# Two-branch image kernel: the first unit's second half moves from GpSimd to VectorE, and the last unit's residual into the output sums

## The chip, the cores and the metric

One NeuronCore of one Trainium2 chip runs the whole kernel. The metric is device time in microseconds (us): the time from the start to the end of one execution. In the profile PE is TensorE (PEld its weight load), DVE is VectorE, ACT is ScalarE, POOL is GpSimd, SP is the engine that issues most of the DMAs; a q behind a name means that engine's queue or sequencer.

## The reference

The input x is (4, 96, 128, 128) in float32. Two residual steps follow each other, each on a group-normalised copy (32 groups of 3 channels):

```
x = x + L0(gn(x))   # layer norm over channels, 1x1 q/kv, depthwise 3x3, channel attention, 1x1 projection
x = x + L1(gn(x))   # 1x1, 3x3, 5x5 and dilated 3x3 convolutions, concatenated, 1x1 fuse back to 96 channels
```

The second step is linear between the norm and the sum. The kernel folds its five weights into one 5x5 convolution of 96 by 96 channels. gn(v) is (v - m) / sqrt(s + eps), m and s being the mean and variance of a group over the image.

## The kernel before

The four images run one after the other. For each image the phases are: projection of the normed rows (L772, float32 matmuls), depthwise convolution as band matrices (L793 to L795), gram products and softmax, the attention output (L855) added to X by DVE (L1432), the statistics of the new X, and then the folded 5x5 convolution in 11 units of rows (L924, L919). X, the image in float32, lies in SBUF all the time.

The convolution is a fast (Toom-Cook-like) form: a unit is 12 rows (4 blocks of 3; the last unit has 8 rows), and its rows are turned into five "points" (planes of a block, two column kinds each) by differences of rows. The points are 4, 3, 1, 0 and 2 in the order of the matmuls. Points 3 and 4 are the first half ("part 0" in the code), points 0, 1 and 2 the second half ("part 1"). For each half there are the planes themselves ("plain") and sums of neighbouring columns ("sums"). Each value is split into a high float16 part (made by ACT, function highs, L1122 and L1127, copied once more by L1116 and L1117) and a low float16 part (made by DVE, lows, L1554 for unit 0 and L1557 for the others). DMAs then place the low parts in further partitions: place_first (L371 to L374, L360 to L362) for unit 0, copy_block (L384) and place_low (L440 to L443, L360 to L362) for the later ones.

Unit 0 is special, since it waits for the second group norm. The mean and variance come from sums over the image: DVE's additions L1432 give the sum, ACT's squares L1085 the sum of squares. Then a chain of single-column instructions on DVE, two 96x1 matmuls on PE (L753: the mean over a group, then the variance) and a root on ACT (L962) give the scale SA and shift SBI (L1487, L1488). So as not to wait for them, the row differences of unit 0 are made from X itself before the scale is known (a difference of rows needs no mean), and the scale enters when the halves are rounded to float16. Who makes them before the change:

- POOL (first_planes, helper take at L632 and column_sums at L628) makes the differences and all points of blocks 1 to 4, first half and second half, and the column sums. Then, once DVE has laid the rows of block 0 less their mean (first_block_rows, L1445, counted in s_pl0), POOL makes the second half of block 0 too. s_fp counts POOL's steps, 24 an image.
- DVE makes block 0's first half (L1450, L1455), adds twice the mean back to the one plane where it doesn't cancel (L1460) and makes the remaining column sums (L1465, L1468).
- ACT then rounds: part 0 plain when s_pl0 is at 4, part 0 sums at s_pl0 6 and s_fp 11, part 1 plain at s_fp 23, then the copies of part 0, part 1 sums at s_fp 24, the normed rows of unit 1 (rows_normed, L1103), and the copies of part 1.
- DVE makes the low parts of part 0 (plain, sums) and part 1 (plain, sums), the x3 and x1 of line L1554. SP places part 0 after the second of them and part 1 after the fourth.
- PE starts unit 0 when its high parts (s_h at 5) and part 0's placed tiles are there.

Next DVE makes unit 1's points (planes: L1511, L1508, L1518, L1519, L1514, L1515, L1536), which needs ACT's normed rows, and its low parts, which need all of unit 0's placing DMAs to be done (s_firstp, s_firstlo), as its buffer is reused. Unit 1's first point on PE leaves its matmuls with the placed low parts for last (L919); they wait for place_low's DMAs.

From unit 2 on DVE, ACT, POOL (differences, L680), SP and PE run in a loop of windows, one unit each. A unit's output: ACT copies the first point (L1166), DVE adds the others from PSUM into acc with their factors (first_rows L1587, last_rows L1605; s_acc counts 11 steps a unit), then adds pairs of kinds into the output buffer ob (outputs, L1618: first the middle row, then the outer rows), POOL adds X (residual, L670, counted in s_res), and SP writes ob out (write_out, L452). The middle outputs wait until the write of the unit before has landed (s_out). After the last unit the next image's projection begins on PE with nothing between.

## Time and profile before

| what | value |
|---|---|
| median of 3 runs | 1725.4 us (1724.74 to 1725.86) |
| profiled execution's own time | 1725.26 us |
| its span | 1723.0 us |
| PE, DVE, ACT, POOL busy | 96%, 87%, 59%, 37% of the span |
| granted TensorE clock, mean | 0.975 of full |

The profile shows one execution. Its span is the time from the first to the last instruction or DMA; the device time is 2.3 us more. Times in rows are us from the start of the span. A number in brackets at a row's end is the time that the engine sat idle before it, with what ended that idle time.

### The profile page before, as it was taken

How to read it: one execution, taken by the hardware profiler on the slowest of the kernel's cores; microseconds unless marked ns; L12 is line 12 of the kernel's file. 1: busy time of each engine (PE TensorE's matmuls, PEld its weight loads, DVE VectorE, ACT ScalarE, POOL GpSimd, SP SyncE). 2: the span in 40 equal slices, each digit the busy share in tenths (PEclk: the TensorE clock that was granted, in tenths of full speed). 3: DMA queues.
4: the chain of work that ended last, by engine and by line, in shares of the span. 5: the costliest groups of instructions: out<-in, count | busy, mean ns of one | idle time of the engine just before them, and what ended most of it. 6: DMA issues, size and time to landing. Idle time of an engine off the chain costs nothing.

```text
span 1723.0 us, 39391 instructions
## 1 busy us (share of the span) xinstructions
PE 1645.8 (96%) x13285; PEld 1550.5 (90%) x13285; DVE 1492.8 (87%) x1930; ACT 1011.6 (59%) x1647; POOL 637.2 (37%) x446
## 2 busy tenths in 40 slices
PE   6999989999999997999999999899999999899998
PEld 5989959999999994999999996799999999599998
DVE  6798879999788859999978886999987887799996
ACT  2866667455285657645546666655447565765541
POOL 5799962222381005232247003323227400512232
PEclk9999979999999998999999998899999999799999
DMA  7012115666502201566630220366651121055553
GB/s 190 0 42 61 45 31 126 169 165 171 148 19 57 72 19 39 149 168 177 165 99 14 73 60 1 86 164 174 168 159 46 41 69 38 1 137 132 140 146 95
DMA packets 101181, 166.05 MB, mean 96 GB/s; under 512 B 40010, under 2 KB 74411, under 8 KB 100940
## 3 DMA queue, kind: packets, MB, share of 16 engines
q1 hardware_dynamic: 77932, 138.95, 31.8%
q10 hardware_dynamic: 23168, 26.04, 4.8%
q8 instruction: 47, 0.77, 0.2%
q14 instruction: 34, 0.28, 0.1%
HBM read 52.20 MB, written 25.17 MB: 45 GB/s over the span
## 4 chain that ended last, share of the span: by engine, by line
PE 70%; DVE 12%; issue 11%; ACT 3%; POOL 1%; SPq 1%; DMA 1%; DVEq 1%; ACTq 0%; POOLq 0%
PE ps L924 28%; PE ps L772 12%; PE ps L793 8%; PE ps L795 7%; PE ps L794 7%; PE ps L821 3%; PE ps L855 3%; DVE region L1557 1%; DVE region L1587 1%; DVE region L1508 1%; POOL region L670 1%; PE ps L735 1%; DVE region L1605 1%; PE ps L919 1%; DMA region<-region 1%
## 5 line engine op out<-in xcount | busy, mean ns | idle before, releaser
L924 PE MATMUL ps<-region,W 128*96 128x256 f16 (+4 forms) x7156 | 796.7, 270 | 5.7 <-DMA region<-region 5.7
L924 PEld LDWEIGHTS ps<-region,W 128*96 128x96 f16 (+2 forms) x7156 | 774.9, 122 | 20.6 <-issue 14.1
L1346 DVE TENSOR_TENSOR region<-V,band 128x2322 f32<-128x2322 f32 (+2 forms) x104 | 257.7, 2488 | 59.2 <-PE ps L795 56.1
L1122 ACT ACTIVATE region<-region 96x1584 f16<-96x1584 f32 (+1 forms) x80 | 98.1, 1273 | 311.0 <-DVE region L1519 306.2
L680 POOL TENSOR_TENSOR region<-region 96x528 f32<-96x528 f32 (+1 forms) x72 | 96.4, 1344 | 407.8 <-DVE region L1557 405.8
L793 PE MATMUL ps<-region 128*128 (+1 forms) x1152 | 228.2, 280 | 10.0 <-DVE region L1355 4.4
L795 PE MATMUL ps<-region 128*128 (+1 forms) x1152 | 222.8, 275 | 0.0
L794 PE MATMUL ps<-region 128*128 (+1 forms) x1152 | 222.3, 275 | 0.0
L1587 DVE SCALAR_TENSOR_TENSOR region<-ps,small,region 96x768 f32<-96x768 f32 (+1 forms) x220 | 203.7, 988 | 10.3 <-PE ps L924 8.5
L772 PE MATMUL ps<-proj,region 96*128 96x240 f32 x1024 | 210.1, 368 | 0.5 <-DVE region L1605 0.4
L772 PEld LDWEIGHTS ps<-proj,region 96*128 96x128 f32 x1024 | 195.2, 191 | 14.4 <-issue 1.2
L670 POOL TENSOR_TENSOR region<-region,X 96x1536 f32<-96x1536 f32 (+1 forms) x44 | 124.0, 2818 | 225.2 <-DVE region L1618 225.2
L793 PEld LDWEIGHTS ps<-region 128*128 128x128 f32 x1152 | 174.6, 192 | 16.5 <-issue 14.8
L599 POOL TENSOR_TENSOR region<-region,cbias 128x576 f32 (+1 forms) x124 | 175.7, 1417 | 34.8 <-DVE region L1320 30.6
L1557 DVE TENSOR_TENSOR region<-region 96x792 f16<-96x792 f32 (+6 forms) x160 | 175.1, 1153 | 0.9 <-DMA region<-region 0.8
L795 PEld LDWEIGHTS ps<-region 128*128 128x128 f32 x1152 | 174.9, 192 | 0.0
L794 PEld LDWEIGHTS ps<-region 128*128 128x128 f32 x1152 | 174.9, 192 | 0.0
L632 POOL TENSOR_TENSOR region<-X 96x512 f32<-96x512 f32 (+1 forms) x16 | 29.2, 1844 | 385.3 <-PE ps L855 385.3
L1014 ACT ACTIVATE region<-ps 128x768 f32 (+1 forms) x80 | 65.8, 822 | 136.9 <-PE ps L795 136.9
L1116 ACT ACTIVATE region<-region 96x1584 f16<-96x1584 f16 (+2 forms) x88 | 114.1, 1296 | 0.0
L1618 DVE TENSOR_TENSOR region<-region 96x256 f32<-96x256 f32 (+3 forms) x176 | 88.4, 543 | 22.5 <-DMA out_dram<-region 20.9
L974 ACT ACTIVATE region<-X,small 96x512 f32 (+1 forms) x128 | 101.6, 802 | 8.1 <-issue 7.3
(208 smaller groups left out, 2229.6 us busy)
## 6 DMA issues: line engine op xcount, KB each, us to landing
region<-region SPq DMA_DIRECT2D x116, 247.5 KB, 4.0
region<-in_x_dram SPq DMA_DIRECT2D x128, 192.0 KB, 2.4
out_dram<-region SPq DMA_DIRECT2D x40, 576.0 KB, 4.2
region<-region ACTq DMA_DIRECT2D x72, 247.5 KB, 2.4
X<-in_x_dram SPq DMA_DIRECT2D x30, 576.0 KB, 5.9
region<-region SPq DMA_DIRECT2D x36, 247.4 KB, 4.9
X<-in_x_dram SPq DMA_DIRECT2D x19, 384.0 KB, 11.1
region<-region SPq DMA_DIRECT2D x24, 185.6 KB, 3.8
```

The lines of the kernel that those rows point to most:

```text
L599: pool.tensor_tensor(Q[:, :, bass.ds(t * AR, AR)].rearrange("p c r -> p r c"), pq[:, i], cbias[:].unsqueeze(1).broadcast_to([P, AR, CO]), ...
L670: pool.tensor_tensor(ob[:, 0:r * W], ob[:, 0:r * W], X[:, bass.ds(u * UR * W, r * W)], ALU.add).then_inc(s_res, 1)
L772: last = mm(ps[:, 2 * i + r // 2, r % 2 * 256:r % 2 * 256 + NP], y1[:, i, r * W:(r + 1) * W], proj[:], start=True, stop=True)
L793: mm(o, T[:, i, 3 * c + 1, 0:W], src, start=True, stop=False)
L794: mm(o[:, 1:H], T[:, i, 3 * c, 0:W], src[:, 0:H - 1], start=False, stop=False)
L795: last = mm(o[:, 0:H - 1], T[:, i, 3 * c + 2, 0:W], src[:, 1:H], start=False, stop=True)
L924: last = mm(o, w, src, start=k == 0, stop=k == len(steps) - 1, skip_group_check=split and ck > 0)
L974: act.activation(y1[:, i, :], X[:, bass.ds(t * BANK, BANK)], ACT.Identity, bias=col(SBIX), scale=col(SAX)).then_inc(s_y1, 1)
L1116: act.activation(hi2[0:C, a:e, x:z], hi[0:C, a:e, x:z], ACT.Copy).then_inc(s_h, 1)
L1346: v.tensor_tensor(T[:, i, 3 * c:3 * c + m].rearrange("p m (i j) -> p m i j", j=3), taps.broadcast_to([P, m, BW // 3, 3]), mask.broadcast_t ...
L1557: v.tensor_tensor(low[:, :, x:end], src, hi[0:C, a:e, x:end], ALU.subtract).then_inc(s_l, 1)
L1587: step = lambda dst, g, factor, src: v.scalar_tensor_tensor(row(dst), product(i, g, blocks), col(factor), row(src), ALU.mult, ALU.add).the ...
```

## The change

1. POOL makes only the differences of unit 0, the first half's points of blocks 1 to 4 and their column sum: 13 steps an image instead of 24. The calls of point_0_and_inf and the column sums of the second half are gone, and with them everything that POOL did for block 0.
2. DVE makes the second half for all five blocks: block 0's difference (second_part_edge, 96x396) between the scale and the low parts of part 0; then, after the low parts of part 0, two scalar_tensor_tensor of 96x660 and one tensor_tensor of 96x990 (second_part), as it does for the later units; then the low parts of part 1.
3. The addition of twice the mean to one plane moves from DVE (L1460) to ACT, after its last squares, as an activation with the new column MG2 as its bias, which DVE makes with one more 96x1 instruction.
4. ACT's copies of part 0 come ahead of part 1's plain rounding, and PE waits for 4 high steps instead of 5.
5. For the last unit of an image X is added by DVE to the two output kinds of acc (three tensor_tensor, between first_rows and middle_outputs) instead of by POOL to ob, and SP writes the rows when DVE's last output step is done.

```diff
--- before.py
+++ after.py
@@ -244,7 +244,7 @@
         SUM, SQ, SHIFT, SPARE, MEAN2, NSH = 31, 32, 33, 34, 35, 36
         OSC_MHALF, OSC_MSIXTH, OSC_SIXTH, OSC_THIRD, OSC_THIRDS, OSC_HALF = range(37, 43)
         QKS, CLAMP, WMAX, TMAX, BMAX = 43, 44, 45, 46, 47
-        MEANX, VARX, SAX, SBIX = 23, 24, 27, 28
+        MEANX, VARX, SAX, SBIX, MG2 = 23, 24, 27, 28, 29
         OSCS = ((OSC, 1.0), (OSC_MHALF, -0.5), (OSC_MSIXTH, -1.0 / 6), (OSC_SIXTH, 1.0 / 6), (OSC_THIRD, 1.0 / 3),
                 (OSC_THIRDS, 2.0 / 3), (OSC_HALF, 0.5))
 
@@ -301,6 +301,7 @@
         s_y2 = sem("normed_rows")
         s_fp = sem("first_unit_rows_by_pool")
         s_pl0 = sem("first_unit_rows_by_vector")
+        s_fix = sem("first_unit_mean_returned")
         s_zero = sem("zero_rows")
         s_pl = sem("row_planes")
         s_eta = sem("neighbour_differences")
@@ -317,9 +318,10 @@
         s_t1 = sem("first_point_copied")
         s_acc = sem("output_steps")
         s_res = sem("residual_added")
+        s_pre = sem("last_unit_residual_added")
         s_out = sem("output_written")
         NPL, NH, NL, NCV, NACC = 8, 8, 4, 5, 11
-        NFP, NPL0 = 24, 6
+        NFP, NPL0 = 13, 9
 
         later = lambda b, u: b * (UNITS - 1) + u
         s_wt = plain_sem("weights_placed")
@@ -337,7 +339,7 @@
         N_DIAG, N_RNK, N_NMX, N_ATT, N_MBLK = (N_AFFN + k for k in (3, 6, 11, 13, 14))
         SETS = AT // 4
         N_MEAN2 = N_MBLK + 3
-        N_VG2, N_AFF2 = N_MEAN2 + 6, N_MEAN2 + 8
+        N_VG2, N_AFF2 = N_MEAN2 + 7, N_MEAN2 + 9
         NST, NPST = N_AFF2, 7
         block = ctx.enter_context(nc.Block())
 
@@ -448,7 +450,10 @@
 
                 r = LASTR if u == UNITS - 1 else UR
                 rows = slice(u * UR, u * UR + r)
-                sync.wait_ge(s_res, b * UNITS + u + 1 + START)
+                if u == UNITS - 1:
+                    sync.wait_ge(s_acc, (b + 1) * UNITS * NACC + START)
+                else:
+                    sync.wait_ge(s_res, b * (UNITS - 1) + u + 1 + START)
                 sync.dma_start(out[bass.ds(b, 1), :, rows, :].rearrange("o c h w -> (o c) (h w)"), ob[:, 0:r * W]).then_inc(s_out, 16)
                 with sync.If(b < B - 1):
                     sync.dma_start(X[:, u * UR * W:(u * UR + r) * W],
@@ -617,28 +622,14 @@
                     slots = lambda x, end, c: pln[:, 1:5, x * RW:end * RW] \
                         .rearrange("p k (t c j) -> p k t c j", c=2, j=PC)[:, :, :, c, 1:1 + HC]
                     plane = lambda k, end, x: pln[:, k:end, x * RW:(x + 1) * RW]
-                    twice = f32at(Y2F_AT + YF * RW, 5 * RW).rearrange("p (k e) -> p k e", k=5)
+                    twice = f32at(Y2F_AT + YF * RW, 4 * RW).rearrange("p (k e) -> p k e", k=4)
 
                     def done(n):
                         pool.wait_ge(s_fp, b * NFP + n + START)
 
-                    def column_sums(k, end, x, y):
-                        pairs = pln[:, k:end, x * RW:y * RW].rearrange("p k (q e) -> p k q e", e=RW)
-                        dst = cs[0][:, k:end, 0:PC] if x == 3 else cs[1][:, k:end]
-                        pool.tensor_tensor(dst.rearrange("p k (q j) -> p k q j", j=PC), pairs[:, :, :, PC:RW],
-                                           pairs[:, :, :, 1:1 + PC], ALU.add).then_inc(s_fp, 1)
-
                     def take(dst, a, d):
                         pool.tensor_tensor(dst, a, d, ALU.subtract).then_inc(s_fp, 1)
 
-                    def point_0_and_inf(k, end, n):
-                        done(n)
-                        take(twice[:, k:end], plane(k, end, 1), plane(k, end, 0))
-                        take(plane(k, end, 2), plane(k, end, 2), plane(k, end, 1))
-                        done(n + 2)
-                        take(plane(k, end, 0), twice[:, k:end], plane(k, end, 0))
-                        take(plane(k, end, 2), plane(k, end, 2), plane(k, end, 1))
-                        done(n + 4)
                     pool.wait_ge(s_x1, b * SETS * 2 + 2 + START)
                     pool.wait_ge(s_o, (b * SETS + 2) * AR + START)
                     for c in range(2):
@@ -646,23 +637,17 @@
                     pool.memset(pln.rearrange("p k (q j) -> p (k q) j", j=PC)[:, :, 0:PC:PC - 1], 0.0).then_inc(s_fp, 1)
                     pool.memset(yb, 0.0).then_inc(s_fp, 1)
                     done(3)
-                    take(twice[:, 1:5], plane(1, 5, 4), plane(1, 5, 3))
+                    take(twice, plane(1, 5, 4), plane(1, 5, 3))
                     done(5)
-                    take(plane(1, 5, 3), twice[:, 1:5], plane(1, 5, 3))
+                    take(plane(1, 5, 3), twice, plane(1, 5, 3))
                     for n in (8, 10):
                         for c in range(2):
                             take(slots(4, 5, c)[:, :, 0], slots(4, 5, c)[:, :, 0], taps(1, c, 1)[:, :, 0])
                         done(n)
-                    column_sums(1, 5, 3, 4)
+                    pool.tensor_tensor(cs[0][:, 1:5, 0:PC], plane(1, 5, 3)[:, :, PC:RW], plane(1, 5, 3)[:, :, 1:1 + PC],
+                                       ALU.add).then_inc(s_fp, 1)
                     for c in range(2):
                         take(slots(0, 3, c), taps(2, c, 3), taps(0, c, 3))
-                    point_0_and_inf(1, 5, 13)
-                    column_sums(1, 5, 0, 3)
-                    pool.wait_ge(s_pl0, b * NPL0 + 1 + START)
-                    own = yb.rearrange("p r e -> p (r e)")
-                    take(pln[:, 0, 0:3 * RW], own[:, 2 * RW:], own[:, 0:3 * RW])
-                    point_0_and_inf(0, 1, 19)
-                    column_sums(0, 1, 0, 3)
 
                 def residual(u, r):
 
@@ -692,8 +677,8 @@
                 pool.wait_ge(s_zero, b + 1 + START)
                 for half in range(2):
                     differences(UNITS - 1, UNITS - 1, half)
-                for u in range(UNITS - 3, UNITS):
-                    residual(u, LASTR if u == UNITS - 1 else UR)
+                for u in range(UNITS - 3, UNITS - 1):
+                    residual(u, UR)
 
         @block.tensor
         def _(pe):
@@ -870,7 +855,7 @@
                         if g == 0:
                             if first:
                                 pe.wait_ge(s_wt, NPLACES * 16)
-                                pe.wait_ge(s_h, n * NH + 5 + START)
+                                pe.wait_ge(s_h, n * NH + 4 + START)
                                 pe.wait_ge(s_firstp[0], (b + 1) * FIRSTP + START)
                             else:
                                 pe.wait_ge(s_dup[1 - i], (b * 5 + k2 + i) * DUP + START)
@@ -1094,6 +1079,11 @@
                     act.wait_ge(s_x1, (b * SETS + k + 1) * 2 + START)
                     squared(k, 0, 1, k + 1)
                 squared_halves(SETS - 1, SETS)
+
+                one = buffers(0)[2][:, 1:5, 4 * RW:5 * RW].rearrange("p k (c j) -> p k c j", c=2)[:, :, :, 1:1 + HC]
+                act.wait_ge(s_fp, b * NFP + 10 + START)
+                act.wait_ge(s_st, sv + N_MEAN2 + 2 + START)
+                act.activation(one, one, ACT.Identity, bias=col(MG2)).then_inc(s_fix, 1)
                 deviation(N_PPRE + b * NPST + 7, 7, 1)
 
                 def rows_normed(u, whole):
@@ -1126,15 +1116,16 @@
                         src = cs[part]
                         act.activation(dst[0:C, a:e, z:end], src, ACT.Copy, scale=1.0 if whole else col(SA)).then_inc(s_h, 1)
                     if whole == 0:
-                        act.wait_ge(s_pl0, b * NPL0 + 4 + START)
+                        act.wait_ge(s_pl0, b * NPL0 + 3 + START)
+                        act.wait_ge(s_fix, b + 1 + START)
                         plain(hi, 0)
-                        act.wait_ge(s_pl0, b * NPL0 + 6 + START)
+                        act.wait_ge(s_pl0, b * NPL0 + 5 + START)
                         act.wait_ge(s_fp, b * NFP + 11 + START)
                         sums(hi, 0)
-                        act.wait_ge(s_fp, b * NFP + 23 + START)
+                        copied(0, 2)
+                        act.wait_ge(s_pl0, b * NPL0 + 8 + START)
                         plain(hi, 1)
-                        copied(0, 2)
-                        act.wait_ge(s_fp, b * NFP + 24 + START)
+                        act.wait_ge(s_pl0, b * NPL0 + 9 + START)
                         sums(hi, 1)
                         midway()
                         copied(1, 6)
@@ -1455,17 +1446,30 @@
                     v.scalar_tensor_tensor(plane0(0, 3, 4), plane0(0, 3, 4), -2.0, plane0(0, 4, 5),
                                            ALU.mult, ALU.add).then_inc(s_pl0, 1)
 
-                    dve.wait_ge(s_fp, b * NFP + 10 + START)
-                    one = pln0[:, 1:5, 4 * RW:5 * RW].rearrange("p k (c j) -> p k c j", c=2)[:, :, :, 1:1 + HC]
-                    v.tensor_scalar(one, one, col(MG), col(MG), ALU.add, ALU.add).then_inc(s_pl0, 1)
-
                 def first_sums():
 
-                    first_done(4)
+                    first_done(3)
                     v.tensor_tensor(cs0[0][:, 0, 0:PC], plane0(0, 3, 4)[:, PC:RW], plane0(0, 3, 4)[:, 1:1 + PC],
                                     ALU.add).then_inc(s_pl0, 1)
+                    dve.wait_ge(s_fix, b + 1 + START)
                     one = pln0[:, :, 4 * RW:5 * RW]
                     v.tensor_tensor(cs0[0][:, :, PC:2 * PC], one[:, :, PC:RW], one[:, :, 1:1 + PC], ALU.add).then_inc(s_pl0, 1)
+                def second_part_edge():
+
+                    own = yb.rearrange("p r e -> p (r e)")
+                    v.tensor_tensor(plane0(0, 0, 3), own[:, 2 * RW:], own[:, 0:3 * RW], ALU.subtract).then_inc(s_pl0, 1)
+
+                def second_part():
+
+                    slot = lambda k: pln0[:, :, k * RW:(k + 1) * RW]
+                    first_done(6)
+                    dve.wait_ge(s_fp, b * NFP + 13 + START)
+                    v.scalar_tensor_tensor(slot(0), slot(0), -2.0, slot(1), ALU.mult, ALU.add).then_inc(s_pl0, 1)
+                    v.scalar_tensor_tensor(slot(2), slot(1), -2.0, slot(2), ALU.mult, ALU.add).then_inc(s_pl0, 1)
+                    first_done(8)
+                    pairs = pln0[:, :, 0:3 * RW].rearrange("p k (q e) -> p k q e", e=RW)
+                    v.tensor_tensor(cs0[1].rearrange("p k (q j) -> p k q j", j=PC), pairs[:, :, :, PC:RW],
+                                    pairs[:, :, :, 1:1 + PC], ALU.add).then_inc(s_pl0, 1)
                 yn = buffers(1)[3]
                 v.memset(col(MG), 0.0)
                 dve.wait_ge(s_x1, (b + 1) * 2 * SETS + START)
@@ -1474,6 +1478,7 @@
                 v.memset(yn.rearrange("p r (c j) -> p (r c) j", c=2)[:, :, 0:PC:PC - 1], 0.0)
                 dve.wait_ge(s_pst, pst + 6 + START)
                 link(st, v.tensor_copy(col(MG), ps[0:C, 7, 0:1]))
+                link(st, v.tensor_scalar(col(MG2), col(MG), 2.0, None, ALU.mult))
                 link(st, v.tensor_tensor(col(DEV), col(MEAN2), col(MG), ALU.subtract))
                 link(st, v.tensor_tensor(col(VAR), col(SHIFT), col(SHIFT), ALU.mult))
                 link(st, v.scalar_tensor_tensor(col(VAR), col(DEV), col(DEV), col(VAR), ALU.mult, ALU.subtract))
@@ -1566,7 +1571,7 @@
                         dve.wait_ge(s_h, n * NH + high + START)
                         low_of(z, end, cs[part])
                     if whole == 0:
-                        plain(part, (1, 3)[part])
+                        plain(part, (1, 5)[part])
                         sums(part, (2, 6)[part])
                     else:
                         plain(1, 1)
@@ -1639,8 +1644,10 @@
                     first_rows(m, i, BPU)
                 dve.wait_ge(s_st, sv + N_AFF2 + START)
                 dve.wait_ge(s_split, N_SPLIT)
-                for part in range(2):
-                    lows(0, 0, 0, 0, part)
+                second_part_edge()
+                lows(0, 0, 0, 0, 0)
+                second_part()
+                lows(0, 0, 0, 0, 1)
                 planes(1, 1)
                 lows(1, 1, 0, 1)
                 first_rows(0, 0, BPU)
@@ -1652,6 +1659,13 @@
                 last_rows(UNITS - 2, 1, BPU)
                 outer_outputs(UNITS - 2, BPU)
                 first_rows(UNITS - 1, 2, LASTB)
+                dve.wait_ge(s_acc, (b * UNITS + UNITS - 1) * NACC + 5 + START)
+                rows = X[:, (UNITS - 1) * UR * W:].rearrange("p (r j c) -> p c r j", j=HC, c=2)
+                for r in range(OR):
+                    n = len(range(r, LASTR, OR))
+                    kinds = acc[:, r, 1:3, 0:n * HC].rearrange("p c (k j) -> p c k j", j=HC)
+                    v.tensor_tensor(kinds, kinds, rows[:, :, r:LASTR:OR], ALU.add).then_inc(s_pre, 1)
+                dve.wait_ge(s_pre, (b + 1) * OR + START)
                 middle_outputs(UNITS - 1, LASTB)
                 last_rows(UNITS - 1, 2, LASTB)
                 outer_outputs(UNITS - 1, LASTB)
```

## Rows read from the trace of the kernel before

**Rows 1.** the page, part 1: engine, busy us, share of the span, instructions.

```profile
PE 1645.8 (96%) x13285; PEld 1550.5 (90%) x13285; DVE 1492.8 (87%) x1930; ACT 1011.6 (59%) x1647; POOL 637.2 (37%) x446
```

**Rows 2.** timeline of PE, fourth image: start, us, line, what, count [idle before].

```profile
1502.78 0.48 PE L753 MATMUL ps<-small,gmean 96*96 96x1 f32 x2 [4.82 <-DVE small L1483]
...
1511.51 2.83 PE L924 MATMUL ps<-region,W 128*96 128x256 f16 x24 [1.38 <-DMA region<-region]
...
1534.69 0.64 PE L919 MATMUL ps<-region,W 96*96 96x256 f16 x4 [1.45 <-DMA region<-region]
```

**Rows 3.** timeline of PE, unit 1's L919 in the first and second image.

```profile
288.22 0.60 PE L919 MATMUL ps<-region,W 96*96 96x256 f16 x4
...
703.50 0.64 PE L919 MATMUL ps<-region,W 96*96 96x256 f16 x4 [1.01 <-DMA region<-region]
```

**Rows 4.** timeline of DVE, fourth image, from the mean to unit 1.

```profile
1496.08 0.15 DVE L1476 COPY small<-ps 96x1 f32<-96x1 f32 x1 [0.37 <-PE ps L753]
1496.26 1.24 DVE L1477 TENSOR_TENSOR small<-small 96x1 f32<-96x1 f32 x1
...
1498.81 1.91 DVE L1479 SCALAR_TENSOR_TENSOR small<-small 96x1 f32<-96x1 f32 x1
...
1501.93 0.79 DVE L1483 SCALAR_TENSOR_TENSOR small<-small 96x1 f32<-96x1 f32 x1
...
1503.78 0.21 DVE L1488 SCALAR_TENSOR_TENSOR small<-small 96x1 f32<-96x1 f32 x1
...
1505.65 4.75 DVE L1554 SCALAR_TENSOR_TENSOR region<-region,small 96x1320 f16<-96x1320 f32 x3 [1.11 <-ACT region L1122]
1510.97 1.25 DVE L1554 SCALAR_TENSOR_TENSOR region<-region,small 96x990 f16<-96x990 f32 x1 [0.57 <-ACT region L1127]
1512.96 1.25 DVE L1511 TENSOR_TENSOR region<-region 96x1056 f32<-96x1056 f32 x1 [0.75 <-ACT region L1103]
```

**Rows 5.** line L1477: shortest, median and longest of its four instructions, in ns.

```profile
L1477 DVE TENSOR_TENSOR small<-small x4: 156/1227/1244, 251.5 to 1496.3; 96x1 f32<-96x1 f32 x4
```

**Rows 6.** timeline of POOL, fourth image, the second half's points.

```profile
1493.52 5.24 POOL L632 TENSOR_TENSOR region<-region 96x528 f32<-96x528 f32 x4
1498.84 1.86 POOL L628 TENSOR_TENSOR region<-region 96x792 f32<-96x792 f32 x1
```

**Rows 7.** timeline of SP's queue, fourth image: the placing of units 0 and 1.

```profile
1508.21 0.65 SPq L371 DMA_DIRECT2D region<-region  x1
...
1519.60 3.75 SPq L384 DMA_DIRECT2D region<-region  x6
```

**Rows 8.** groups of instructions with shapes apart: total busy us, mean ns.

```profile
L1514 DVE SCALAR_TENSOR_TENSOR region<-region 96x528 f32<-96x528 f32 x36 | 25.4, 705 | 1.1
...
L1536 DVE TENSOR_TENSOR region<-region 96x990 f32<-96x990 f32 x4 | 4.7, 1186 | 0.4
```

**Rows 9.** ACT: a row of the page's part 5, then its timeline, fourth image.

```profile
L974 ACT ACTIVATE region<-X,small 96x512 f32 (+1 forms) x128 | 101.6, 802 | 8.1 <-issue 7.3
...
1503.30 0.26 ACT L962 ACTIVATE small<-ps,epsc 96x1 f32<-96x1 f32 x1 [5.58 <-PE ps L753]
...
1506.16 1.94 ACT L1122 ACTIVATE region<-region,small 96x1980 f16<-96x1980 f32 x1
```

**Rows 10.** 1506 to 1508 us: PE busy (instructions), granted clock, DMA share, GB/s.

```profile
1506.00:1508.00 2.00, 2.00 (x16) 0.75 0.00 0
```

**Rows 11.** timelines at the end of the third image (DVE), the last (DVE, POOL).

```profile
1298.40 0.63 DVE L1618 TENSOR_TENSOR region<-region 96x192 f32<-96x192 f32 x2 [1.87 <-DMA out_dram<-region]
...
1712.97 0.63 DVE L1618 TENSOR_TENSOR region<-region 96x192 f32<-96x192 f32 x2
...
1715.50 0.81 DVE L1605 SCALAR_TENSOR_TENSOR region<-ps,small,region 96x576 f32<-96x576 f32 x1 [0.91 <-PE ps L924]
1716.35 1.03 DVE L1618 TENSOR_TENSOR region<-region 96x384 f32<-96x384 f32 x2
...
1717.45 2.00 POOL L670 TENSOR_TENSOR region<-region,X 96x1024 f32<-96x1024 f32 x1 [8.53 <-DVE region L1618]
```

## The prediction

> **What bounds the kernel now.** I read the page first: PE is busy for 1645.8 of 1723.0 us [rows 1], so only a stretch where PE waits can give time back, and its timeline shows where. In each image there is one such stretch, between the attention's output and unit 1 of the convolution. PE stands idle 4.82 us before the variance matmul, starts unit 0 at 1511.51, and in the fourth image stops again for 1.45 us in unit 1, at L919, for a DMA [rows 2]. The second image has that stop too (1.01 us); in the first L919 follows without one [rows 3]. The third is as the first. From there to the end of an image PE doesn't wait, so what is gained at that L919 is gained in the image.
>
> What does PE wait for? DVE's timeline answers [rows 4]. The mean arrives at 1496.08 (I call this C), and the scale is finished at 1503.99, where L1488 ends (S): 7.91 us for a chain of 96x1 instructions and a few small ones. Three of them take 1.24 us or more, although the same line has once taken 156 ns [rows 5]. What else runs then is POOL's second half for blocks 1 to 4, from 1493.52 to 1500.70 [rows 6], and block 0's behind it. A two-input instruction of DVE lasts about as long as one of POOL's is under way (5.24 / 4 = 1.31 us; 1.91 beside the column sums' 1.86). So I hold POOL's work to be what stretches the chain.
>
> **The change, part by part.** First the chain from C to S. POOL now ends with the differences, at 1493.5, 2.6 us ahead of C, so nothing overlaps. L1477 and L1478 fall from 1.24 to 0.16, L1479 from 1.91 to 0.22, L1483 from 0.79 to 0.22: 1.08 + 1.08 + 1.69 + 0.57 = 4.4 us back. The new MG2 instruction adds 0.19. C to S becomes 7.9 - 4.4 + 0.2 = 3.7 us, so S comes 4.2 us earlier. One image of the four already escaped one block [rows 5]; it regains some 0.7 less, 3.5. Bounds: nothing (if it isn't POOL) to 4.4.
>
> ACT's addition of 2 MG costs about 0.80 [rows 9]. ACT sits idle for 5.58 us before its root, from 1497.72 [rows 9]; the root would now come at 1499.1, the addition ends at 1498.5. It is hidden, with 0.6 us to spare; uncovered it would cost 0.2 to 0.8 an image. L1460 leaves DVE, but stood beside the root: nothing.
>
> Then unit 0 after S. Until part 0's low parts are done (SP starts placing at 1508.21, S + 4.2 [rows 7]) nothing changes, for the edge difference (96x396, about 0.53, as L1618's 1.03 / 2 for 384 [rows 11]) fits into the 1.11 us for which DVE waits there for ACT [rows 4]. So PE starts unit 0 4.2 us earlier, at 1507.3; the s_h wait of 4 is met at S + 4.3, before the DMAs land.
>
> Part 1 gets longer. At S + 4.13 DVE starts two instructions of 96x660 (705 ns at 528 [rows 8], so 0.85 each, overlapping by 0.08) until S + 5.8, then the sums of 96x990, 1.19 [rows 8], until S + 7.0. ACT's plain rounding, 1.94 [rows 9], can begin only at S + 5.85 and ends at S + 7.8, its sums (half as many elements) at S + 8.8; DVE's low parts follow, 2.25 for the plain (the third of the x3, from 4.75) and 1.25, and end at S + 11.35. Before, they ended at 1512.22, S + 8.23 [rows 4]. So this costs 3.1 us, paid out of 4.2: the end comes 1.1 us earlier.
>
> Unit 1 hangs on that end by two ways. DVE's planes started at 1512.96, 0.75 late for ACT's normed rows [rows 4]; now these are there first (S + 10.8), and that wait goes. By this way unit 1's low parts start 1.75 us earlier. The other way is the placing of part 1: copy_block, which waits for it, began at 1519.60 [rows 7], 7.4 us after the end; with the same 7.4 it gives only 1.1 to 1.5 earlier (SP, which was still issuing part 0 then, is free now, and that is worth up to 0.6). I take 1.6 us for three images and 1.0 for the one with less to regain. What then comes is unchanged: low parts, ten placing DMAs, L919. Sum: 3 x 1.6 + 1.0 = 5.8 us. PE's own 4.2 don't pass: it reaches L919 early and stands there, 1.45 + 4.2 - 1.6 = 4.1 us in the fourth image, 2.6 us or so in the first.
>
> In the first image L919 had no wait, but its DMA was just in time (the last is issued as late after the low parts as in the second), so the same 1.6 goes for it.
>
> The last unit. Three additions of 96x384, 96x384 and 96x256: 0.52 + 0.52 + 0.4 [rows 11], a little more for X's stride, 1.5 us. Inside the run they stand in the 1.87 us for which DVE waits for the earlier write [rows 11]: 0, between -0.3 and 0. POOL's addition went on beside the next image's projection: 0 too. In the last image DVE has no such wait at 1712.97; middle outputs move to 1714.5 and end at 1715.1, and of the two L1605 the second starts at about 1715.85 instead of 1715.50, since it waited 0.91 us for PE [rows 11]. The outer outputs end at 1717.7 instead of 1717.38, and SP's last write goes out then instead of after POOL's addition, at 1719.45. Gain 1.7 us; bounds 0.5 (nothing hidden) to 2.1.
>
> Sum: 5.8 + 1.7 = 7.5. The profiled execution took 1725.26 us (1723.0 of it the span), 0.14 below the median of 1725.4; 1725.4 - 7.5 = 1717.9 us.
>
> **The rule that speaks against it.** The granted clock was 0.75 in 1506 to 1508 [rows 10], between its levels of 1.2 and 2.4 GHz: it rose at about 1507, 4.2 us after PE's work had begun again at 1502.78, behind 4.82 us of idle [rows 2]. The new stop at L919 is up to 4.1 us long in the middle of full-rate work; the stops that are there now, 1.38 and 1.45 us [rows 2], are followed by matmuls at the full rate (24 of 256 columns in 2.83 us). The Trainium skill ("TensorE: Matmul & The Clock Gate", § HAM oscillation) says that an idle stretch of PE puts it back to half rate, and that this bites where a burst waits for DMAs. By that rule the second rival below would be true, by the rows until now it isn't.
>
> **The rivals.** Two tenths of a per cent, 3.4 us, is about what can be told from no change.
>
> - The clock falls in the new stop. Each time some 4.2 us of unit 1 run at half rate, which loses 2.1 us. In two images: 1717.9 + 4.2 = 1722.1; in all four 1726.3, no change. For: the stop grows by 2.4 to 2.6 us. Against: none after the stops of 1.4 us. 15 of 100, mostly with one or two falls.
> - DVE's longer half is all that is felt, and the time is slower. Place: DVE from C to the low parts of part 1. If not POOL's instructions but something else stretches the 96x1 ones, S moves 0.2 later, part 1 costs its 3.1 less the 0.75 that the normed rows give back, so 2.6 an image: 10.4 - 1.7 = 8.7, 1734 us. It decides as soon as less than about 2.2 of the 4.2 us come back. For: nothing but that the overlap is inferred. Against: 156 ns in one image. 4 of 100.
> - PE's 4.2 us pass whole, as unit 1's placing isn't what L919 needs: 3 x 4.2 + 3.5 + 1.7 = 17.8, 1707.6 us. Against: the DMA named in front of L919 in two images. 4 of 100.
> - The overlap comes back but not the end (the write's landing, not the outputs, sets it; or the additions stick out in three images): 1719.5 to 1720. 12 of 100.
> - The change does nothing it says, as POOL ends later than C. It ends 2.6 us before. 2 of 100: 1725.
>
> My forecast has the other 63. The range of 8 in 10 runs from 1713.5 (unit 1 by 2.4 each, as the DMAs find SP free) to 1722.5 (two falls of the clock). Faster by over 0.2%, so below 1722.0: 63 + 12 + 4 and some of the first rival, less the tails, 0.82. Within 0.2%: 0.13. Slower: 0.05.
>
> **What would show it.** After the change L1477 to L1483 must be 0.15 to 0.22 us each, and C to the end of L1488 3.7 us. POOL has nothing between 1493.5 and unit 2's differences. DVE's last low part ends 11.35 us after S. PE starts unit 0 4.2 us earlier against C, and L919 of unit 1 shows a wait of 2.3 to 4.1 us with a DMA before it, at full granted clock. The last 20 us show three additions of 0.4 to 0.55 us and a write issued right behind L1618. It is wrong if those one-column instructions stay over 1 us, if unit 1's stop is gone, or if the granted clock reads 0.5 in unit 1.

## The result, and the profile after

The changed kernel takes 1713.25 us (median of 4 runs, 1711.75 to 1713.73) against 1725.12 of the kernel before: a ratio of 0.9929, interval 0.9912 to 0.9946, so 11.9 us less. The forecast was 1717.9, with 7.5 us of gain and a range down to 1713.5. The direction and the mechanism came as forecast, the gain is half as large again, and the time lies 0.25 us under the range. That last distance is small beside the noise: the interval of the ratio is 9.3 to 15.2 us of gain.

DVE's timeline of the fourth image (start, us, engine, line, operation, operands, count, idle before):

```profile
1488.64 0.15 DVE L1480 COPY small<-ps 96x1 f32<-96x1 f32 x1 [0.37 <-PE ps L738]
1488.83 0.15 DVE L1481 TENSOR_SCALAR small<-small 96x1 f32<-96x1 f32 x1
1489.01 0.15 DVE L1482 TENSOR_TENSOR small<-small 96x1 f32<-96x1 f32 x1
...
1489.39 0.22 DVE L1484 SCALAR_TENSOR_TENSOR small<-small 96x1 f32<-96x1 f32 x1
...
1492.04 0.15 DVE L1493 SCALAR_TENSOR_TENSOR small<-small 96x1 f32<-96x1 f32 x1
...
1493.80 2.41 DVE L1559 SCALAR_TENSOR_TENSOR region<-region,small 96x1320 f16<-96x1320 f32 x2 [0.58 <-ACT region L1112]
1496.13 0.84 DVE L1467 SCALAR_TENSOR_TENSOR region<-region 96x660 f32<-96x660 f32 x1
1496.89 0.83 DVE L1468 SCALAR_TENSOR_TENSOR region<-region 96x660 f32<-96x660 f32 x1
1497.76 1.19 DVE L1471 TENSOR_TENSOR region<-region 96x990 f32<-96x990 f32 x1
1499.74 3.44 DVE L1559 SCALAR_TENSOR_TENSOR region<-region,small 96x1980 f16<-96x1980 f32 x2 [0.80 <-ACT region L1112]
1503.21 1.25 DVE L1516 TENSOR_TENSOR region<-region 96x1056 f32<-96x1056 f32 x1
...
1510.83 4.49 DVE L1562 TENSOR_TENSOR region<-region 96x1584 f16<-96x1584 f32 x4 [0.53 <-DMA region<-region]
```

The one-column instructions that took 0.79 to 1.91 us in [rows 4] last 0.15 to 0.22. From the mean C (1488.64) to the end of the scale S (1492.19) it is 3.55 us, where it was 7.91. The two points and the sums of the second half are new between the two L1559; the last low part ends at 1503.18, and the planes of unit 1 follow at once, without the 0.75 us for ACT. POOL is done before C, with L631 as the last:

```profile
1481.69 4.34 POOL L631 TENSOR_TENSOR region<-X 96x768 f32<-96x768 f32 x2
1515.48 2.58 POOL L665 TENSOR_TENSOR region<-region 96x528 f32<-96x528 f32 x2 [29.45 <-DVE region L1562]
```

PE's timeline of the same image answers to [rows 2]:

```profile
1491.04 0.48 PE L738 MATMUL ps<-small,gmean 96*96 96x1 f32 x2 [0.52 <-DVE small L1488]
...
1499.57 2.83 PE L909 MATMUL ps<-region,W 128*96 128x256 f16 x24 [0.17 <-issue]
...
1520.49 4.49 PE L909 MATMUL ps<-region,W 128*96 128x256 f16 x24 [1.85 <-DMA region<-region]
1524.82 0.61 PE L904 MATMUL ps<-region,W 96*96 96x256 f16 x4
```

Unit 0 starts 10.93 us after C instead of 15.43. The stop that was in front of unit 1's late matmuls (those with the placed low parts, now L904) stands in this image in front of unit 1 itself, at 1520.49, since its first tiles are not placed either. In the first three images it is split between the two places. And the end of the run (DVE, then SP's queue), to be read beside [rows 11]:

```profile
1703.08 1.36 DVE L1667 TENSOR_TENSOR region<-region,X 96x384 f32<-96x384 f32 x3
1704.48 0.63 DVE L1623 TENSOR_TENSOR region<-region 96x192 f32<-96x192 f32 x2
1705.21 1.54 DVE L1610 SCALAR_TENSOR_TENSOR region<-ps,small,region 96x576 f32<-96x576 f32 x2
1706.78 1.03 DVE L1623 TENSOR_TENSOR region<-region 96x384 f32<-96x384 f32 x2
...
1707.97 0.32 SPq L457 DMA_DIRECT2D out_dram<-region  x1
```

**Where the 11.6 us between the two spans lie.** All from the two traces, in us after each image's C:

| image | S, before / after | last low part of unit 0 ends | unit 1's low parts begin | unit 1's late matmul | gain |
|---|---|---|---|---|---|
| 1 | 7.89 / 3.55 | 16.13 / 14.53 | 24.00 / 21.71 | 36.89 / 34.51 | 2.4 |
| 2 | 7.21 / 3.54 | 15.45 / 14.54 | 23.74 / 21.92 | 37.46 / 35.72 | 1.7 |
| 3 | 7.89 / 3.55 | 16.13 / 14.54 | 24.23 / 21.71 | 38.33 / 34.42 | 3.9 |
| 4 | 7.91 / 3.55 | 16.14 / 14.54 | 24.03 / 22.19 | 38.61 / 36.18 | 2.4 |

That is 10.46 us. From the late matmul to the next image's C it was 377.8, 376.5 and 377.8 us and is 378.6, 376.5 and 379.0: 2.07 are given back, in the first and third image. The end of the run (from the fourth late matmul) gives 1.77, and the first image's C came 1.46 us earlier, at 249.87 instead of 251.33. 10.46 - 2.07 + 1.77 + 1.46 = 11.6. The 1.46 arise in the first 60 us, where the program is the same in both; e2 and e5 below, which have the changed first unit too, have C at 251.22 and 251.05. It is chance of these two executions; how much of it is in the medians no trace tells. Without it the traces account for 10.2 us.

### The profile page after: what moved, and what is told of

Read it like the earlier page. It is cut to its first block, busy times and chain, and to the rows that moved or that the text cites. A ratio compares the mean times of both kernels' runs of the same rounds, so it can differ in the third digit from the quotient of the medians.

```text
span 1711.4 us, 39369 instructions
## 1 busy us (share of the span) xinstructions
PE 1653.8 (97%) x13285; PEld 1555.2 (91%) x13285; DVE 1491.1 (87%) x1958; ACT 1015.3 (59%) x1651; POOL 584.5 (34%) x398
## 4 chain that ended last, share of the span: by engine, by line
PE 73%; DVE 11%; issue 8%; ACT 3%; DMA 2%; SPq 2%; DVEq 1%; POOL 1%; ACTq 0%; POOLq 0%
PE ps L909 30%; PE ps L757 12%; PE ps L778 8%; PE ps L780 7%; PE ps L779 7%; PE ps L806 3%; PE ps L840 3%; DVE region L1562 2%; DMA region<-region 1%; DVE region L1592 1%; DVE region L1513 1%; DVE region L1610 1%; PE ps L720 1%; PE ps L904 1%; DVE region L1623 1%
## 5 line engine op out<-in xcount | busy, mean ns | idle before, releaser
L1592 DVE SCALAR_TENSOR_TENSOR region<-ps,small,region 96x768 f32<-96x768 f32 (+1 forms) x220 | 203.7, 988 | 10.2 <-PE ps L909 8.4
L655 POOL TENSOR_TENSOR region<-region,X 96x1536 f32<-96x1536 f32 x40 | 116.1, 2902 | 192.8 <-DVE region L1623 192.8
L631 POOL TENSOR_TENSOR region<-X 96x512 f32<-96x512 f32 (+1 forms) x16 | 29.2, 1853 | 385.3 <-PE ps L840 385.3
## 6 DMA issues: line engine op xcount, KB each, us to landing
X<-in_x_dram SPq DMA_DIRECT2D x19, 384.0 KB, 10.5
```

The source lines that it names most:

```text
L655: pool.tensor_tensor(ob[:, 0:r * W], ob[:, 0:r * W], X[:, bass.ds(u * UR * W, r * W)], ALU.add).then_inc(s_res, 1)
L1592: step = lambda dst, g, factor, src: v.scalar_tensor_tensor(row(dst), product(i, g, blocks), col(factor), row(src), ALU.mult, ALU.add).the ...
```

## The experiments

Each was timed beside the kernel before on the same chip; ratios are to that, with the 95% interval.

**The two halves of the change apart.** e1 is the kernel before with only the last unit's part (`write_out`'s wait, POOL's loop one unit shorter, the three additions with s_pre). e2 is the changed kernel with that part taken back.

```diff
 # e1, against the kernel before
-                for u in range(UNITS - 3, UNITS):
-                    residual(u, LASTR if u == UNITS - 1 else UR)
+                for u in range(UNITS - 3, UNITS - 1):
+                    residual(u, UR)
...
+                    v.tensor_tensor(kinds, kinds, rows[:, :, r:LASTR:OR], ALU.add).then_inc(s_pre, 1)
```

> The kernel before with only the last unit's part of the change. My theory: only the very end of the run gains, 1.7 us (the two traces differ by that much after the last late matmul), so 1723.4 us against 1725.1; the three inner image boundaries stay as they are. Rival: the additions also free something at each boundary (POOL's last addition gone), 0.5 us or more each, so 3.2 us or more, 1721.9 or less.

Measured: 1722.62 us, 0.9986 (0.9977 to 0.9996) of 1725.52: 2.4 us, interval 0.7 to 4.0. From the fourth late matmul to the end the trace shows 1.8 us less than before. The time can't exclude the rival's 3.2, the trace does: from each late matmul to the next image's C it is no shorter than before (378.2, 377.0, 378.0).

> The changed kernel with the last unit's residual back on POOL. My theory: 8 to 10 us are the first unit's, so 1715 to 1717 us. Rival (the end is worth more than 1.7): over 1717.5. With e1 the sum of both should give the 11.9 us of the whole change to within 1 us; if it falls short, part of the 11.9 is chance between executions, such as the 1.5 us by which the two traces already differ before the first depthwise matmul, where the program is the same.

Measured: 1715.08 us, 0.9939 (0.9926 to 0.9953): 10.5 us. The sum with e1, 12.9, agrees with the whole change's 11.9 (9.3 to 15.2). So some 10 us are the first unit's and about 2 the end's.

**Is it POOL that stretches the chain?** e3 keeps the changed kernel's order, and lets POOL go on with work that nobody needs; ACT's last sums wait for it, so that its scratch is free in time.

```diff
 # e3, in first_planes, behind the last differences
+                    for k in range(6):
+                        done(13 + k)
+                        pool.tensor_tensor(f32at(Y2F_AT + YF * RW, 4 * RW), X[:, 0:4 * RW], X[:, 4 * RW:8 * RW], ALU.subtract).then_inc(s_fp, 1)
```

> The changed kernel, but POOL goes on after its 13 steps with six two-input instructions of 96x528 (7.9 us, read from X, written to scratch), so that it is busy while DVE runs the chain of one-column instructions. Theory (POOL's instructions hold up DVE's two-input ones): the three after the mean take 1.2 to 1.9 us again instead of 0.15 to 0.22, the mean to the scale takes 7.5 to 8 us instead of 3.55, the low parts of part 1 end 4 us later, and some 3 us per image are lost: 1725 us, no better than before. Rival (the gain is from the shorter order of work, not from POOL being still): chain stays 3.6 us, 1713 us.

Measured: 1726.51 us, 1.0011 (1.0001 to 1.0020): all of the gain is gone. The chain is stretched again, and DVE makes the second half as well. DVE and POOL of the fourth image:

```profile
1499.53 1.17 DVE L1486 TENSOR_TENSOR small<-small 96x1 f32<-96x1 f32 x1
1500.73 0.16 DVE L1487 TENSOR_TENSOR small<-small 96x1 f32<-96x1 f32 x1
1500.93 1.15 DVE L1488 SCALAR_TENSOR_TENSOR small<-small 96x1 f32<-96x1 f32 x1
...
1503.83 1.06 DVE L1492 SCALAR_TENSOR_TENSOR small<-small 96x1 f32<-96x1 f32 x1
```

```profile
1496.60 8.28 POOL L653 TENSOR_TENSOR region<-X 96x528 f32<-96x528 f32 x6
```

Three of the four take 1.06 to 1.17 us, nearly as long as one POOL instruction (8.28 / 6 = 1.38 us); L1487 takes 0.16, so I suppose that it fell between two of them. C to S is 6.93 to 6.95 us in all four images. I had expected 7.5 to 8; POOL's work ends here at 1504.88, before S (1506.11), and no DVE instruction behind it is long. The late matmul comes 3.3 to 3.5 us later than in the changed kernel in each image, as much as S. So what S gains or loses reaches unit 1 whole; the second half on DVE is a separate term.

e4 asks what POOL must do to be in the way: two memsets instead. DVE waits for them before part 0's low parts and before the second half, both behind S.

```diff
 # e4, at the same place
+                    pool.memset(cs[1], 0.0).then_inc(s_fp, 1)
+                    pool.memset(buffers(0)[1], 0.0).then_inc(s_fp, 1)
```

> The changed kernel, but POOL goes on after its 13 steps with two memsets, of 96x990 and 96x2475 (3.6 us together, until about 1.5 us after the mean): POOL is busy, but reads nothing. If it is any POOL instruction that holds DVE up, the first two-input instruction after the mean takes over 1 us again. If it must be one that reads SBUF, all stay at 0.15 to 0.22 us and the mean to the scale stays at 3.55 us.

Measured: 1715.52 us, but in a single run, so the reading rests on the trace: C to S is 3.55 in all four images. POOL's second memset runs from 1488.37 to 1492.61, longer than I had reckoned, and so beside the first 2.4 us of DVE's chain (C is 1490.20 here):

```profile
1488.37 4.24 POOL L652 MEMSET region<- 96x4950 f16 x1
```

```profile
1490.58 0.16 DVE L1485 TENSOR_TENSOR small<-small 96x1 f32<-96x1 f32 x1
1490.77 0.15 DVE L1486 TENSOR_TENSOR small<-small 96x1 f32<-96x1 f32 x1
1490.96 0.21 DVE L1487 SCALAR_TENSOR_TENSOR small<-small 96x1 f32<-96x1 f32 x1
```

Nothing is held up. So it isn't POOL being busy. What e3's instructions do and the memset doesn't is read SBUF (the operation differs too; no run separates the two). The Trainium skill ("SBUF — State Buffer", § SBUF: two separate sides) says that it is the reading: the port pair that both share is locked for whole instructions, and a DVE instruction with two SBUF inputs is in conflict only with a GpSimd one that reads SBUF. Both traces agree.

**The small parts.** e5 puts the addition of twice the mean back on DVE (`v.tensor_scalar(one, one, col(MG), col(MG), ALU.add, ALU.add).then_inc(s_fix, 1)` at the end of first_part, ACT's activation gone).

> The changed kernel with the addition of twice the mean back on DVE (0.69 us, behind the first half's point), ACT's activation gone. Theory: DVE waits 0.53 us for ACT's root at that place, so only 0.1 to 0.2 us of the addition stick out per image: mean to scale 3.65 to 3.75 us, 1713.5 to 1714 us. Rival (moving it to ACT is part of the gain): 0.6 us or more per image, 1716 us.

Measured: 1713.95 us, 0.9939 (0.9923 to 0.9956), which overlaps the changed kernel's interval; C to S is 3.55 in all four. The addition took 0.54 us and stands wholly in the wait for the root (0.53 in the changed kernel). The move to ACT brought nothing to the chain.

e6 gives ACT its old order back.

```diff
 # e6, in highs; PE waits for n * NH + 5, DVE's plain(1) for 3
-                        copied(0, 2)
                         act.wait_ge(s_pl0, b * NPL0 + 8 + START)
                         plain(hi, 1)
+                        copied(0, 2)
```

> The changed kernel, but ACT keeps the old order: it rounds part 1 before it copies part 0, and PE waits for 5 high steps. Theory (unit 1 hangs on DVE's last low part and ACT's normed rows): ACT waits until the scale + 5.6 us before the copies, so its sums and normed rows come 2.0 us later, the last low part 0.8 later, the planes of unit 1 1.4 later; 1.4 us per image lost, 1719 us. PE starts unit 0 2.1 us later, and that alone costs little, since it stands before unit 1 anyway. Rival (order on ACT doesn't matter, only POOL's silence does): 1713.3 us.

Measured: 1717.23 us, 0.9961 (0.9947 to 0.9975): by the ratios 3.8 us slower than e5, which ran beside it and stands for the changed kernel: 1.0 an image. The two intervals overlap a little; the traces say the same. ACT's timeline of the fourth image:

```profile
1500.32 1.95 ACT L1112 ACTIVATE region<-region,small 96x1980 f16<-96x1980 f32 x1 [3.25 <-DVE region L1468]
1502.18 1.29 ACT L1106 ACTIVATE region<-region 96x1320 f16<-96x1320 f16 x1
```

ACT stands still for 3.25 us where it now does the copies. Against the changed kernel the last low part comes 0.65 us later (0.8 expected), unit 1's planes 1.4 later (C + 15.95), as expected, and the late matmul 1.2, 1.2, 1.3 and 0.3 later. The path is the expected one, the price nearly a third under it.

**What does the second half on DVE cost?** e7 cuts its three instructions to two elements each and lets POOL fill the sums with zeros: points 0 and 2 of unit 0 are not computed.

```diff
 # e7, in second_part
-                    v.scalar_tensor_tensor(slot(0), slot(0), -2.0, slot(1), ALU.mult, ALU.add).then_inc(s_pl0, 1)
+                    few = lambda k: slot(k)[:, 0:1, 0:2]
+                    v.scalar_tensor_tensor(few(0), few(0), -2.0, few(1), ALU.mult, ALU.add).then_inc(s_pl0, 1)
```

> The changed kernel with the second half's two points and column sums on DVE cut to two elements each, the sums filled with zeros by POOL: 2.8 us of DVE's work left out per image (points 0 and 2 of unit 0 are not computed). This measures what the second half on DVE costs. Theory (the chain to unit 1 runs through it, until ACT's copies of part 0 bound it at the scale + 4.3): last low part 1.2 us earlier, 1.1 us per image gained, 1709 us. Rival (it is hidden): 1713 us; rival (all 2.8 us pass): 1702 us.

Measured: 1708.11 us, 0.9907 (0.9891 to 0.9924): by the ratios 5.5 us under e5, 1.4 an image; by the late matmuls 1.0 to 1.6. The last low part ends at S + 9.62 instead of 10.99. So of the 2.8 us about half are on the path; the other half are hidden, by the theory behind ACT's copies.

**A version that beats both.** If DVE's last low part is the path, the points should be made where DVE waits. e8 makes block 0's difference during the wait for the root, and the two points behind the first sums, ahead of part 0's low parts; the column sums stay between the parts. ACT then finds the points ready and keeps the old order.

```diff
 # e8, against the changed kernel (ACT's order and the counts as in e6)
                 first_part()
+                second_part_edge()
...
-                second_part_edge()
+                second_points()
                 lows(0, 0, 0, 0, 0)
-                second_part()
+                second_sums()
```

> A version meant to beat both: the edge difference goes into DVE's wait for the root, the second half's two points come right behind the first sums (where DVE waits 0.58 us for ACT), ahead of part 0's low parts; only the column sums stay between the parts. ACT keeps the old order, as it can now round part 1 at the scale + 2.4 us. Theory: part 0's low parts end 0.55 us later (PE starts unit 0 that much later, which costs nothing), the last low part ends at the scale + 9.1 instead of 11.0, so unit 1's late matmul comes 1.4 to 1.9 us earlier per image, where PE itself (start + 21.5 us) then bounds it: 1706 to 1708 us. Rival (unit 1 is bound by the placing DMAs' traffic and not by when they start): 1712 to 1713 us.

Measured: 1705.60 us (1704.54 to 1706.20), 0.9890 (0.9873 to 0.9906) of the kernel before: 19 us less, and its slowest run is 5.5 us below the changed kernel's fastest. DVE, fourth image:

```profile
1486.06 0.56 DVE L1460 TENSOR_TENSOR region<-region 96x396 f32<-96x396 f32 x1
1486.68 0.16 DVE L1496 RECIPROCAL small<-small 96x1 f32<-96x1 f32 x1
...
1487.50 0.84 DVE L1467 SCALAR_TENSOR_TENSOR region<-region 96x660 f32<-96x660 f32 x1
1488.26 0.83 DVE L1468 SCALAR_TENSOR_TENSOR region<-region 96x660 f32<-96x660 f32 x1
1489.01 2.40 DVE L1563 SCALAR_TENSOR_TENSOR region<-region,small 96x1320 f16<-96x1320 f32 x2
1491.33 1.18 DVE L1474 TENSOR_TENSOR region<-region 96x990 f32<-96x990 f32 x1
1492.43 3.43 DVE L1563 SCALAR_TENSOR_TENSOR region<-region,small 96x1980 f16<-96x1980 f32 x2
```

DVE doesn't wait from the reciprocal to the last low part; that ends at S + 8.8. The late matmul is at C + 34.31, 33.90, 34.02 and 34.41, 1.05 earlier in the mean, which is 4.2 us of the 7.65 against the changed kernel. From it to the next C it is 376.3, 376.6 and 377.8 us, so that what the changed kernel gave back, and 1.5 more in the first image, is kept: another 3.4. The rival, that the traffic of the placing bounds unit 1 at 1712 to 1713 us, is out. In the first and third image the last placing DMA has landed at C + 32.4 and 32.6, so PE itself is now last there; in the second and fourth it is still the DMA (33.9 and 34.4).

## Why the prediction was wrong

- What bounds it: right. All of the gain but the end's lies between C and unit 1. That "what is gained at that L919 is gained in the image" holds only in part: of 10.46 us 2.07 are given back behind it.
- The chain from C to S: right. Forecast 3.7 us, measured 3.55; the cause, which was inferred from the durations, is shown by e3 and, as to what POOL must be doing, narrowed by e4. (Of the "three" that took 1.24 us or more one, L1478, took 1.23.)
- ACT's addition hidden, L1460 worth nothing: right (e5).
- PE starts unit 0 4.2 us earlier and stands at unit 1 instead: right in kind (10.93 after C instead of 15.43). The stop was forecast at the late matmuls alone, 2.3 to 4.1 us long; it came before unit 1 as well as there, 0.5 to 2.2 us in all.
- **The step that failed is the sum for unit 1, "3 x 1.6 + 1.0 = 5.8 us"; it measured 10.5**, 8.4 net of what is given back later. It was mis-sized in three places. The last low part came 0.5 us an image earlier than the forecast C + 15.05 (C + 14.54): ACT could round part 1 at S + 5.57 and not 5.85, and C to S was 0.15 shorter, which are most of it. Unit 1's low parts then began 2.1 us earlier in the mean, 0.7 more than forecast, 0.5 of it that same half microsecond (and the forecast's 1.1 + 0.75 is 1.85, not its 1.75). And the late matmul gained 2.6 in the mean, another 0.5, where the forecast said "What then comes is unchanged". From the end of unit 1's low parts to the late matmul it took 8.4, 9.2, 9.6 and 10.1 us before and 8.3, 9.3, 8.2 and 9.5 now. In the third image that is 1.4 us, and there the forecast's "its DMA was just in time", carried over by "The third is as the first", is false. The trace before has the last placing DMA landed at C + 36.90 and the late matmul at C + 38.33: PE came last, having stood 1.09 us at unit 0's own late matmuls, and the DMA had 1.4 us of slack. In the first image the two are at 36.70 and 36.89, just in time indeed. So PE's gain passed in the third until the DMA became the bound (landed at 34.38, late matmul at 34.42), and that image gained 3.9 us and not 1.6. A missing wait shows that the other side was in time, not that it was only just in time; for such an image the bounds were 1.6 to 4.2, and I took the low end as the value, from the first image's schedule, which I had not compared with the third's.
- The end of the run: 1.7 forecast; 1.8 in the traces of the changed kernel and of e1, and e1's 2.4 (0.7 to 4.0) doesn't contradict. The three additions take 1.36 us.
- The fall of the clock, the first rival in the list ("the second" in the paragraph above it): it happened, in one image of the four. The granted clock in the fourth image (columns: length, PE busy and count, clock, DMA share, GB/s):

```profile
1518.00:1520.00 2.00, 0.64 (x5) 1.00 1.13 273
1520.00:1522.00 2.00, 1.51 (x11) 0.82 0.86 179
1522.00:1524.00 2.00, 2.00 (x11) 0.50 0.31 64
1524.00:1526.00 2.00, 2.00 (x17) 0.83 0.00 0
```

After 1.85 us of standing still the clock goes to the lower of its levels, and the 24 matmuls at 1520.49 take 4.49 us instead of 2.85. That costs at most 1.6 us, and less where the late matmul would have waited for its DMA anyway. My price of 2.1 a fall was near, my place and count of falls too pessimistic. The rule of the Trainium skill ("TensorE: Matmul & The Clock Gate", § HAM oscillation) holds here in its kind, a burst that waits for DMAs loses the rate, but not for each such stop (see the last section).

- The rival of the full pass (17.8 us) was too sweeping, but true in part for the third image; a chance of 4 in 100 for it, with a range that ended at 2.4 us an image, was too little.
- Luck: 1.46 us of the difference between the two traces is chance (above). Without it they come to 10.2 us, still 2.7 over the forecast, and nearly all of that is the unit 1 term.

Still open: why 0.8 and 1.2 us are given back after unit 1 in the first and third image. The traces show where, not why. In the first image PE stops 0.82 us for ACT's copy of a unit's first point (L1157), 44.3 us after the late matmul; e2 to e5 have the same stop (0.83 to 0.85), the kernel before and e6 to e8 don't. In the third PE's weight loads wait for that copy in one unit after another, 0.06 to 0.22 us each, which the kernel before and e8 don't have, and PE stops 0.26 us for DVE before the next image's projection. ACT is late there against PE; what makes it late no run tells apart.

## What to carry to other kernels

Where one-column instructions of VectorE take over a microsecond, look for a two-input GpSimd instruction beside them: moving it away was worth more than the 2.8 us of work that VectorE took over. Then place the work that was taken over into waits that are already there; that was worth two thirds of the change once more (e8). And where an engine shows no wait at a merge of two paths, look up when the other path arrived (here the landing of the last DMA); if that can't be had, write its slack down as unknown and carry it into the range upward too.

## What the runs showed of the hardware

A GpSimd memset of 4.24 us held up none of VectorE's two-input instructions; beside subtractions of 96x528 read from SBUF 96x1 instructions of 0.15 to 0.22 us took up to 1.17 us in e3, and 1.91 in the kernel before beside the 1.86 us of L628. The clock's fall depends on more than the length of one stop: it came after stops of 1.85 us (above) and, in e8's first image, of 1.92 us, but not after the first image's 1.85 us in the kernel before, nor after 2.48, 2.60 and 2.78 us before unit 0 in e6's first three images. e6's third image, PE (the granted clock is 1.00 from 1088 to 1092 us, and the 24 matmuls take 2.83 us):

```profile
1089.46 2.83 PE L909 MATMUL ps<-region,W 128*96 128x256 f16 x24 [2.78 <-ACT region L1107]
```

e8's first image, PE and then the granted clock:

```profile
261.69 4.14 PE L909 MATMUL ps<-region,W 128*96 128x256 f16 x24 [1.92 <-DMA region<-region]
```

```profile
264.00:266.00 2.00, 2.00 (x11) 0.50 0.84 206
```
